# Storing the normed rows block by block ahead of the expert weights, and holding back the next layer's loads

## What is computed

```python
x = x + delta_rule_attention(layernorm(x))        # layer 0, attention
x = x + experts(layernorm(x), gate_w, up_w, down_w)   # layer 0: 8 experts, top 2, silu(x g) * (x u), then down
x = x + softmax_attention(layernorm(x))           # layer 1, 16 heads, rope
x = x + postnorm_experts(layernorm(x), W1, b1, Wo)    # layer 1: 8 experts, top 1, gelu, a shared Wo
```

## Time and profile before

| what | before |
|---|---|
| median of 3 runs (lowest to highest) | 886.75 us (884.74 to 889.0) |
| the profiled execution: its time | 886.98 us |
| the profiled execution: its span | 885.7 us |
| mean granted PE clock | 0.905 of full speed |
| PE, DVE, ACT, POOL busy | 82%, 75%, 58%, 27% of the span |

### The profile page before, as it was taken

How to read it: one execution, slowest core, us unless ns; L and a number is a source line. 1 busy time by engine, 2 the same in 40 slices (tenths; PEclk the granted TensorE clock), 3 DMA queues, 4 the chain that set the end, 5 groups by cost and what they waited for, 6 DMA issues and landing times. The chain is left out here.

```text
span 885.7 us, 18662 instructions
## 1 busy us (share of the span) xinstructions
PE 726.3 (82%) x7088; PEld 354.2 (40%) x7088; DVE 668.1 (75%) x1333; ACT 513.5 (58%) x1012; POOL 237.6 (27%) x295
## 2 busy tenths in 40 slices
PE   6999968988519999909787999999999999946880
PEld 3343236643319999905111222222222222235770
DVE  7878975456874555557986999999999998954555
ACT  3754522565523444454246888888888888933553
POOL 0130010304027666351741200000000000006763
PEclk9999989987658999968658999999999999977995
DMA  3440010000291112133875030404120000033113
GB/s 98 101 91 3 1 23 5 5 3 0 78 332 53 49 46 49 29 104 97 228 160 184 3 85 2 85 3 86 31 57 1 3 2 2 11 95 107 52 48 98
DMA packets 40336, 55.56 MB, mean 63 GB/s; under 512 B 12264, under 2 KB 27760, under 8 KB 39608
## 3 DMA queue, kind: packets, MB, share of 16 engines
q1 hardware_dynamic: 36280, 46.24, 19.7%
q0 software_dynamic: 3968, 8.13, 3.4%
HBM read 35.41 MB, written 14.75 MB: 57 GB/s over the span
## 5 line engine op out<-in xcount | busy, mean ns | idle before, releaser
L1032 DVE TENSOR_REDUCE arena<-psum 128x1 f32<-128x1024 f32 x256 | 300.7, 1216 | 23.9 <-PE psum L916 21.2
L1171 ACT ACTIVATE arena<-psum 128x512 f32<-128x512 f32 x512 | 265.9, 605 | 53.7 <-PE psum L935 53.6
L916 PE MATMUL psum<-arena 56*128 56x512 bf16 x512 | 178.9, 409 | 11.8 <-DVE arena L1032 10.2
L935 PE MATMUL psum<-arena 59*128 59x512 bf16 x512 | 155.8, 388 | 5.9 <-ACT arena L1171 3.7
L946 PE MATMUL psum<-arena 128*32 128x512 f32 x1024 | 138.1, 611 | 8.7 <-issue 8.7
L369 PE MATMUL psum<-arena 128*128 128x128 f32 x808 | 107.1, 279 | 0.4 <-DVE arena L420 0.4
L935 PEld LDWEIGHTS psum<-arena 59*128 59x128 bf16 x512 | 38.4, 94 | 166.2 <-ACT arena L1171 140.9
L369 PEld LDWEIGHTS psum<-arena 128*128 128x128 f32 x808 | 101.1, 197 | 0.7 <-DVE arena L420 0.7
L485 POOL DMA_INDIRECT rows_y<-arena x62 | 61.8, 997 | 39.8 <-DVE arena L434 34.9
L1240 POOL TENSOR_SCALAR arena<-arena 128x16 f32<-128x16 f32 x16 | 4.1, 254 | 249.2 <-DVE arena L1032 249.0
L396 PE MATMUL psum<-arena 128*128 (+1 forms) x496 | 66.6, 277 | 3.3 <-ACT arena L464 2.6
(11 more groups left out here) (312 smaller groups left out, 1048.4 us busy)
## 6 DMA issues: line engine op xcount, KB each, us to landing
arena<-scr_k SPq DMA_DIRECT2D x15, 448.0 KB
arena<-scr_q SPq DMA_DIRECT2D x15, 448.0 KB
arena<-in_f_up SPq DMA_DIRECT2D x1, 4096.0 KB, 13.5
arena<-rows_y SPq DMA_DIRECT2D x12, 256.0 KB, 4.5
scr_q<-arena SPq DMA_DIRECT2D x6, 384.0 KB, 3.3
arena<-in_f_down SPq DMA_DIRECT2D x1, 2048.0 KB, 19.9
rows_x<-xn SPq DMA_DIRECT2D x2, 1024.0 KB, 14.8
arena<-in_f_up SPq DMA_DIRECT2D x1, 2048.0 KB, 9.5
```

The costliest lines, as they stand in the source:

```text
L916: mm = pe.matmul(ps[:, bank + half, :], q[rows, k, h, (qh * 4 + qt) * P:(qh * 4 + qt + 1) * P], kk[rows, k, h, half * BLK:(half + 1) * BLK ...
L935: pe.matmul(ps[:, score_bank(n), :], kk[0:KA, k, h, kb * P:(kb + 1) * P], q[0:KA, k, h, qh * BLK:(qh + 1) * BLK], start=True, stop=True).t ...
L1032: dve.tensor_reduce(mx[:, qh, h * 4 + qt:h * 4 + qt + 1], ps[:, bank:bank + 2, :].rearrange("p a b -> p (a b)"), X, ALU.max).then_inc(S("a ...
L1171: act.activation(pt[:, (u % 3) * HG + h, :], ps[:, score_bank(n), :], ACT.Exp, scale=float(HD) ** -0.5).then_inc(S("a1_exp"), 1)
```

## The change

In f0, the one store of all rows becomes four stores, one for each block, each issued when its block is normed, and they stand between the up and the down weights in SP's order. The 11 attention loads are issued only after the eighth gather has landed. In f1, the store becomes two: blocks 0 to 2 before the barrier that ends the attention, and block 3 as the first thing behind the barrier, ahead of the five small loads and the weights. The waits on `_rows` count the new stores (64 and 32 instead of 16).

```diff
-    pool.wait_ge(S(name + "_rows"), 16)
+    pool.wait_ge(S(name + "_rows"), c.rows)
...
-def rows_out_sp(c, name, k, rows=NT):
-
-    c.sp.wait_ge(c.sem("n_row"), NT * c.turn + rows)
-    c.sp.dma_start(c.rows_x[k].rearrange("(p t) d -> p t d", p=P), c.mem["xn"][:]).then_inc(c.sem(name + "_rows"), 16)
+def rows_out_sp(c, name, k, blocks):
+
+    at = slice(blocks[0] * TPB, (blocks[-1] + 1) * TPB)
+    c.sp.dma_start(c.rows_x[k].rearrange("(p t) d -> p t d", p=P)[:, at, :], c.mem["xn"][:, at, :]).then_inc(c.sem(name + "_rows"), 16)
 
 
 def ffn0_sp(c, w):
-    for name in ("up", "down"):
-        c.sp.dma_start(c.mem["e_" + name][:], w["f0_" + name]).then_inc(c.sem("f0_weights"), 16)
-    c.weights = 32
-    rows_out_sp(c, "f0", 0)
+    c.sp.dma_start(c.mem["e_up"][:], w["f0_up"]).then_inc(c.sem("f0_weights"), 16)
+    for n in range(NB):
+        c.sp.wait_ge(c.sem("n_row"), NT * c.turn + TPB * (n + 1))
+        rows_out_sp(c, "f0", 0, range(n, n + 1))
+    c.sp.dma_start(c.mem["e_down"][:], w["f0_down"]).then_inc(c.sem("f0_weights"), 16)
+    c.weights, c.rows = 32, 16 * NB
+    c.sp.wait_ge(c.sem(f"f0_landed{GATHERED - 1}"), 16)
     attn1_loads(c, w)
     results_sp(c, "f0", 2, c.rows_y[0])
...
     c.weights = 48
-    rows_out_sp(c, "f1", 1, 2 * TPB)
     results_sp(c, "f1", 1, c.rows_y[1])
...
-    dve.wait_ge(S("f1_rows"), 16)
+    dve.wait_ge(S("f1_rows"), c.rows)
...
     tables_sp(c, w, "f1", 1)
+    c.sp.wait_ge(c.sem("n_row"), NT * (c.turn + 1) + TPB)
+    c.sp.wait_ge(c.sem("a1_nrow"), 2 * TPB)
+    rows_out_sp(c, "f1", 1, range(3))
...
     c.turn = 3
     c.release()
+    c.sp.wait_ge(c.sem("n_row"), NT * c.turn + 2 * TPB)
+    rows_out_sp(c, "f1", 1, range(3, NB))
+    c.rows = 32
     ffn1_memory(c, w)
     ffn1(c, w, x, out)
```

## The result

| what | before | after |
|---|---|---|
| median (lowest to highest), 22 runs each | 888.07 us (884.74 to 893.61) | 886.22 us (883.69 to 888.82) |
| ratio after to before | | 0.9971, 95% interval 0.9958 to 0.9985 |
| profiled execution: span | 885.7 us | 886.1 us |
| mean granted PE clock | 0.905 | 0.892 |

The ratio is worth 2.6 us (888.07 x 0.0029), with an interval of 1.3 to 3.7; the medians alone lie 1.85 apart. The forecast was 4.5, so the direction was right and the size was not. The two profiled spans can't be compared as a whole: layer 0's experts begin at 237.50 us in one and at 238.85 in the other, and nothing ahead of that was changed. I therefore read each expert layer from its own first DVE instruction, L128 in f0 (root of the variance of all rows) and L668 in f1 (L666 before).

What follows compares the result with a forecast made beforehand. First gathers bound by the rows' store, f0's landing by attention loads, then f0 by PE and f1 by POOL's gathers. Gains 2.8 (f0) + 1.7 (f1) = 4.5 us off 886.98: 882.5, median 882.3; range 879.8 to 886.4.

Steps and rivals of the forecast that it cites:

- the stores' move: f0's start: with the rows stored ahead of down, the first gather follows the index alone; gain 0 to 0.6 us.
- The 0.56 that no row explained: f0's first gather: part of its 0.84 us lag behind the store's landing; might vanish or stay.
- The loads held back: f0's start: with the DMA idle, gather to first transposition takes 2.69 instead of 5.17 us; gain 2.48.
- What that start wins reaches the end of f0.: f0 after the first transposition: a fixed amount of PE work follows, so the start's gain of 2.5 to 3.1 us carries through.
- a margin for the second gather: f0's start: gather two follows 1.3 us behind the first; PE returns over 2 us later, its first eight matmuls taking 2.08.
- f0's term: f0's start: first transposition earlier by 2.5 to 3.1 us, taken as 2.8, the middle.
- Forecast 1.7: f1's start: first gather follows the index by 0.28 us, at 800.98 instead of 802.70; lower bound 0.9.
- Covers costed at 0: Both layers: later weights, and in f0 attention loads during the PE-bound part, stay hidden behind other waits; cost 0 us.
- Small stores slow: Rival, f0: four 256 KB stores delay down; 885.6 at 2.3 us each (chance 0.05), about 928 at 13.0 (loss 0.07).
- The estimate of 10.4 us: f0's four stores one after another, by the Trainium skill's transfer costs, against 4.4 us for one; time near 885 to 886.
- Only the rows' part pays: Rival: f0's first gather still takes 5 us, f0 wins 0 to 0.6, total 1.7 to 2.3; 884.7 us, chance 0.14.

Runs made afterwards that it cites:

- f0_rows_only: Kernel before plus only f0's four stores ahead of the down weights; attention loads not held back, f1 as before. Ratio to before 1.0004 (0.9983 to 1.0024).
- f0_held_only: Kernel before plus only f0's attention loads held until the eighth gather landed; one store behind both weights, f1 as before. Ratio to before 0.9983 (0.9959 to 1.0007).
- f1_only: Kernel before plus only the change in f1; f0 as before. Ratio to before 0.9998 (0.9977 to 1.0019).
- after_again: The changed kernel run once more, unaltered, as a base for other runs. Ratio to before 0.9973 (0.9955 to 0.9991), median 883.83 us against 885.49.
- f0_only: Kernel before plus only the change in f0; f1 as before. Ratio to before 0.999 (0.9969 to 1.0011).
- warm_gap: Changed kernel plus idle matmuls filling PE's waits behind the routing and in its middle, both layers. Ratio to before 0.992 (0.9898 to 0.9942).
- before_warm: Kernel before plus 14 (f0) and 12 (f1) idle matmuls filling PE's wait behind the routing. Ratio to before 1.0002 (0.9978 to 1.0025).

## Why the prediction was wrong in size

- **What held the first gather in f0.** The prediction saw index and store level and gave the stores' move 0 to 0.6 us, with half of it in the forecast. For the gather it is 0: with either order of stores it stands 0.88 behind the index. The 0.56 that no row explained was the order of POOL's two waits. The four stores alone did bring the first transposition 1.06 us forward (f0_rows_only), by way of the loads; beside the held-back loads they add nothing that shows.
- **The loads held back.** Right: 5.17 fell to 2.89 us (2.69 forecast), and f0_held_only alone does it.
- **"What that start wins reaches the end of f0." This step failed.** It took the PE work behind the first transposition as a fixed time. It rested on PE being busy for 30 of 30 us at full clock, which holds from 33 us behind the layer's start. Ahead of that PE runs at half clock, so 2.25 us won there carry 1.1. The row that shows it was there: the first eight matmuls at 2.08 us, which I read only as a margin for the second gather. f0's term was 2.8 and came out at 1.1 to 1.3: some 0.55 went because the first transposition moved by 2.25 and not by 2.8, and 1.0 to 1.1 through the half clock.
- **f1.** Forecast 1.7. The profiled pair gives 0.72. Against the four kernels without filling that have f1's old order the gather gains 16.16 - 14.81 = 1.35, and the layer 99.20 - 97.89 = 1.3 (means; new order: f1_only, after, after_again). Three deviations met: the gap of 0.80 instead of 0.28 took 0.5; the index came at 14.0 instead of 13.54 and took another 0.5; and the store before landed later in the other executions (gather at 16.14 to 16.53) than in the one I had (15.54), which gave 0.6 back. The index was late because the router's matmuls ran at half clock, first before, then after:

```profile
787.31 0.86 PE L192 MATMUL psum<-xnT,arena 128*32 128x128 f32 x24 [1.08 <-PEq L2576]
```

```profile
788.29 1.51 PE L192 MATMUL psum<-xnT,arena 128*32 128x128 f32 x24 [1.08 <-PEq L2581]
```

It was at 13.5 in two of the five executions with the old order and in none of thirteen with the new; whether the change has a part in that is not shown.
- **Covers costed at 0.** Right: down at 261.8 is 1.2 us later than forecast and 2.1 us ahead of ACT's copy; f1's weights delay ACT and nobody behind it; the attention's loads are issued at 274.7 to 279.8 and PE stays busy for 16.00 of 16.00 us meanwhile, though the worst gather takes 6.8 us to land instead of 5.0:

```profile
274.00:290.00 16.00, 16.00 (x146) 16.00 (x145) 9.34 (x24) 6.88 (x12) 12.29 (x13) 1.00 0.46 149
```

- **Small stores slow.** No: four of 256 KB in front of down, landing side by side, make it 2.0 us later behind the layer's start (22.95 against 20.95) and cost nothing that anyone waits for. The estimate of 10.4 us, for four stores one after another, did not come about; the figures of the Trainium skill that it used are measured on transfers issued by GpSimd, and SP issues these.
- **A rival that fits by number only.** "Only the rows' part pays" gave 1.7 to 2.3 us, nearer to the measured 2.6 than the forecast. Its mechanism is the wrong way round: in f0 the held-back loads paid and the rows' part did not.

The corrected sum is f0 159.26 against 160.55 us of length (after, f0_only, after_again against before, f1_only), 1.3, and f1 1.3: together 2.6, the measured 2.6. That they meet to 0.1 us is luck: two executions of one kernel differ by 0.3 to 0.4 us in f1's length (after, warm_gap), and the interval of the measured gain is 1.3 to 3.7.

## What to carry to other kernels

Ask at which clock the work runs that a start moves: TensorE work moved earlier within a half-clock stretch keeps only half of the gain unless full clock comes earlier too, and filling a wait with a few idle matmuls moved f0's last scatter by 2.7 us (2.0 us in the timed medians) where the real change moved it by 1.1. It pays only where TensorE sets the pace: in f1 it moved full clock by 7 us and the length hardly at all. Where POOL waits for two events ahead of a gather, try the wait for the one that comes last in first place; and take a position from several executions before a term of a microsecond is built on it.

## What the runs showed of the hardware

- The order of two waits in front of one indirect transfer of POOL is worth 0.5 us: 0.80 to 0.89 against 0.29 to 0.31.
- Full clock came at 33 to 34 us behind f0's start in seven executions whose first transpositions lie 2.4 us apart; in two others at 31.5 and 36.5.
- In f1 of before_warm the clock fell back to half at about 803.8 us, with no wait of PE longer than 1.55 us since the filling.
- Four stores of 256 KB queued behind a 4 MB load each landed in 13.2 us, side by side.
- The first 24 of the router's matmuls at f1's start ran at full clock in some executions and at half clock in others (0.86 against 1.51 us), and the index was at 13.54 or at 14.02 us. before and before_warm, with the same code up to there, had 13.54 and 14.00.
- The kernel before took 885 to 889 us in some sessions and 914 to 919 in others, and chip 4 is among both. The changed kernels' traces show the added time in the two expert layers.
